# A graph and attention layer on one core: token chunks of 512, 512 and 226, counting windows in equal portions, and panel splits moved by one job

## The chip, the core and the metric

The kernel runs on one core of a Trainium2 chip. The time is the device time of one launch in microseconds (us), and lower is better. A core has five engines with queues of their own: TensorE (PE in the profile, with its weight loads shown as PEld), VectorE (DVE), ScalarE (ACT), GpSimd (POOL), and SyncE (SP), which here only issues DMAs. They wait for one another by semaphores. Matrix products go from SBUF to one of eight PSUM banks of 512 fp32 columns, and ACT or DVE take them out.

## What is computed

1250 tokens of 1024 numbers, 20000 edges (`src`, `dst`), fp32 in and out:

```python
xn = _layernorm(x)
x = x + gnn(xn, edge_index, W, b) + mix(xn, Wq, Wk, Wv, Wo, P)
x = x + ffn(_layernorm(x), Wg, Wu, Wd, Wr, temperature)
...
h = xn @ W.T + b                      # gnn: degree-normalised neighbour sum of h
out = segment_sum(norm[:, None] * h[col], row)
...
q', k' = relu(q P.T)/8, relu(k P.T)/8   # mix: 16 heads of 64, linear attention
attn = (q' @ (k'.T @ v)) @ Wo.T + bo
...
h = silu(x @ Wg[e]) * (x @ Wu[e])     # ffn: 8 experts of 128, weights w from a router
out = sum_e w[:, e] * (h @ Wd[e])
```

## The kernel before

**Products.** The tokens are padded to 1280 = 10 tiles of 128 (`NT`). An fp32 operand is kept as two fp32r parts, a high one (`xnH`, `w_hi`: a rounded copy, made by ACT) and a low one (`xnL`, `w_lo`: raw minus high, made by DVE or POOL), and a product is three matmuls for each of 8 slices of 128 rows: high by high, high by low, low by high. So one job that fills a PSUM bank is 24 matmuls. There are two forms. With tokens stationary (`rows`, L1525) the moving operand is 512 weight columns. With weights stationary (`columns`, L1653, and `expert`, L1789) the moving operand is a chunk of tokens, and `CHUNKS` cuts the 1250 tokens into three.

**Stages.** (1) Layer norm and the first value panel with 10 jobs `rows`. (2) Steps 10 to 39, one job `rows` each, for keys and values in two halves: in these steps the edge counts are made too. The 20000 edges are sorted by destination and lie in 157 chunks of 128. Window w of 32 destinations (`NWIN` = 40) takes `SHARE[w]` chunks for certain (25 for window 0, 11 for window 1, down to 3) and the rest, which depends on the data, in a loop (L1265, L1612). For each chunk DVE makes two one-hot matrices (`hot_pair`, L1253: 128x128 and 128x320, fp16) in a ring of 12, and PE multiplies them into bank 6 or 7 (L1608). A finished window is copied by ACT to `cw` (L897), added by POOL to `acc` (L728) and stored by SP. (3) 24 query jobs `columns(("q", j))`, chunk j % 3 each, interleaved with 8 products `fold` and then, from j = 8, with 16 products `mixed(g, h)` of three matmuls, for which Wo's eight row panels are loaded and split. (4) 20 jobs `rows` for H = xn W (`("h", hf, t)`). (5) Mixture and aggregation, 40 jobs with 512 columns. (6) The router and 48 jobs `expert(n, g)`, n = 0 to 23, three chunks for each of 8 experts, gate and up. (7) 20 jobs `down` with 512 columns.

**What sets the order.** Each engine's program is written out by hand. In stage 2 `_window_steps` (L48) deals whole windows to steps 11 to 39: a step takes windows until the chunks done reach its goal. DVE's step is: one-hots of the step's windows, then the result of the step's job (`k_out` or `v_out`), then a fold's low part. PE's is: the job, a fold, the windows, and then `kv` of the tile before. In stage 3 the jobs q and m (or fold) take banks 2 to 4 in turn, and a job waits until the job three before it has been drained (`free_bank`, L1521). ACT's turn j (L944 to L968) is `q_feature(j)`, which copies q_j out (L926) and rounds it (L929), then `m_high` (L942), and after odd j from 9 to 19 `wo_high(g + 2)` (L935), which waits for the DMA that SP issues in the same turn, after `m` has been drained (L497 to L499). POOL's turn is `q_low(j)`, then `wo_low`. H's first panel is split in four pieces after turns 14, 16, 18 and 20 (L854 on ACT, L682 on POOL). The second value panel is split at ACT's steps 10 to 13 and in POOL's call at L723, ahead of the first addition to `acc`.

## Time and profile before

| what | us |
|---|---|
| median of 3 runs | 1137.25 |
| lowest and highest | 1136.33, 1137.45 |
| the profiled execution | 1137.28 |
| its span (first to last instruction) | 1135.3 |
| PE busy | 1109.2 (98%) |
| ACT, POOL, DVE busy | 252.1, 295.7, 369.1 |
| TensorE's granted clock, mean | 0.995 |

The profiled execution took as long as the median of the runs, and 2.0 us of it lie outside the span. PE is busy for nearly the whole span, and a matmul counts as busy until its modelled end, so that several overlap: a busy share of 98% doesn't tell how densely they follow each other. That is read from their start times.

### The profile page before, as it was taken

Reading aid. Unit: us, or ns where it says so; the run is one execution under the profiler, and the core shown is the slowest. Engines: PE = TensorE matmul, PEld = TensorE weight load, DVE = VectorE, ACT = ScalarE, POOL = GpSimd, SP = SyncE. Lnnn points to the kernel's source line nnn. Section 1 sums busy time; section 2 is a strip of 40 time slices with the busy share of each in tenths; the row PEclk is TensorE's granted clock in tenths of the full one; section 3 lists DMA queues with packets and bytes.
Section 4 is the critical chain, followed back from the end, with each engine's and each line's share of the span. In section 5 each row is a group of like instructions: output and inputs, shape, how many; then the busy total and the mean of one; then the engine's idle time right before and its main releaser. Section 6 shows DMA issues by size and latency. Waiting matters only on the chain.

```text
span 1135.3 us, 15415 instructions
## 1 busy us (share of the span) xinstructions
PE 1109.2 (98%) x5707; PEld 955.6 (84%) x5707; DVE 369.1 (33%) x987; ACT 252.1 (22%) x398; POOL 295.7 (26%) x236
## 2 busy tenths in 40 slices
PE   5999999999999989999999999999999999999998
PEld 4885777878889988888878888887999999998887
DVE  6855256555542111142212223344321111111111
ACT  4331111112223234321111112334221111112000
POOL 6001201112123136330032443434132222225000
PEclk9998999999999999999999999999999999999999
DMA  6303001222233476713069996875022222216321
GB/s 238 112 29 102 12 19 53 67 59 63 71 92 103 159 254 226 241 55 149 1 188 298 312 262 192 240 222 159 1 84 60 60 60 60 68 53 213 103 100 67
DMA packets 144518, 139.29 MB, mean 123 GB/s; under 512 B 6636, under 2 KB 120636, under 8 KB 144189
## 3 DMA queue, kind: packets, MB, share of 16 engines
q1 hardware_dynamic: 143868, 136.20, 38.4%
q10 hardware_dynamic: 576, 2.10, 0.5%
q8 instruction: 48, 0.79, 0.3%
q14 instruction: 26, 0.20, 0.1%
HBM read 102.32 MB, written 35.96 MB: 122 GB/s over the span
## 4 chain that ended last, share of the span: by engine, by line
PE 93%; DMA 2%; DVE 2%; ACT 1%; issue 1%; SPq 0%; DVEq 0%; ACTq 0%
PE ps L1534 10%; PE ps L1535 10%; PE ps L1536 10%; PE ps L1800 7%; PE ps L1802 6%; PE ps L1801 6%; PE ps L1742 4%; PE ps L1736 4%; PE ps L1716 3%; PE ps L1717 3%; PE ps L1847 3%; PE ps L1718 3%; PE ps L1846 3%; PE ps L1848 3%; PE ps L1544 3%; PE ps L1659 2%
## 5 line engine op out<-in xcount | busy, mean ns | idle before, releaser
L1534 PE MATMUL ps<-w_hi,xnH 128*128 128x512 f32 x480 | 192.2, 400 | 0.0
L1536 PE MATMUL ps<-w_hi,xnL 128*128 128x512 f32 x480 | 187.9, 391 | 0.0
L1535 PE MATMUL ps<-w_lo,xnH 128*128 128x512 f32 x480 | 187.8, 391 | 0.0
L1534 PEld LDWEIGHTS ps<-w_hi,xnH 128*128 128x128 f32 x480 | 90.8, 189 | 19.7 <-POOL w_lo L682 0.3
L1536 PEld LDWEIGHTS ps<-w_hi,xnL 128*128 128x128 f32 x480 | 90.6, 189 | 19.5
L1535 PEld LDWEIGHTS ps<-w_lo,xnH 128*128 128x128 f32 x480 | 90.8, 189 | 17.7
L728 POOL TENSOR_TENSOR acc<-acc,cw 128x320 f32<-128x320 f32 x40 | 35.7, 892 | 171.5 <-ACT cw L897 170.6
L1659 PE MATMUL ps<-xnH,w_hi 128*128 128x416 f32 (+1 forms) x192 | 69.1, 360 | 3.1 <-DVE mL L1303 3.1
L1800 PE MATMUL ps<-x2H,guH 128*128 128x416 f32 (+1 forms) x192 | 68.1, 355 | 0.4 <-ACT wT L1077 0.4
L1802 PE MATMUL ps<-xnH,guL 128*128 128x416 f32 (+1 forms) x192 | 67.8, 353 | 0.0
L1801 PE MATMUL ps<-x2L,guH 128*128 128x416 f32 (+1 forms) x192 | 67.8, 353 | 0.0
L1801 PE MATMUL ps<-xnL,guH 128*128 128x416 f32 (+1 forms) x192 | 67.8, 353 | 0.0
L1800 PE MATMUL ps<-xnH,guH 128*128 128x416 f32 (+1 forms) x192 | 67.8, 353 | 0.0
L1802 PE MATMUL ps<-x2H,guL 128*128 128x416 f32 (+1 forms) x192 | 67.8, 353 | 0.0
L1661 PE MATMUL ps<-xnH,w_lo 128*128 128x416 f32 (+1 forms) x192 | 67.8, 353 | 0.0
L1660 PE MATMUL ps<-xnL,w_hi 128*128 128x416 f32 (+1 forms) x192 | 67.7, 353 | 0.0
L682 POOL TENSOR_TENSOR w_lo<-w_raw,w_hi 128x1024 fp32r<-128x1024 f32 x16 | 39.3, 2460 | 107.3 <-ACT w_hi L854 106.9
L1489 DVE TENSOR_TENSOR prd<-ps,wB 128x416 f32<-128x416 f32 (+1 forms) x24 | 14.2, 592 | 161.8 <-PE ps L1802 145.2
L1254 DVE TENSOR_SCALAR hot<-iota,key 128x128 f16<-128x128 f16 x178 | 54.6, 307 | 37.0 <-issue 31.6
L778 POOL TENSOR_TENSOR cL<-cR,cH 128x1280 fp32r<-128x1280 f32 x20 | 59.0, 2948 | 23.7 <-ACT cH L991 23.7
L1255 DVE TENSOR_SCALAR hot<-iota,key 128x320 f16<-128x320 f16 x178 | 55.9, 314 | 0.1
L773 POOL TENSOR_TENSOR xh<-xh,bob 128x512 f32<-128x512 f32 x10 | 12.9, 1288 | 135.1 <-DMA bob<-in 94.0
(312 smaller groups left out, 2050.3 us busy)
## 6 DMA issues: line engine op xcount, KB each, us to landing
cR<-c_d SPq DMA_DIRECT2D x20, 640.0 KB, 5.4
foldin<-in SPq DMA_DIRECT2D x32, 256.0 KB, 2.8
guR<-in SPq DMA_DIRECT2D x16, 512.0 KB, 5.4
c_d<-cw SPq DMA_DIRECT2D x40, 160.0 KB
w_raw<-in SPq DMA_DIRECT2D x12, 512.0 KB, 6.6
xb<-in SPq DMA_DIRECT2D x10, 512.0 KB, 4.9
qs0H<-qT_d SPq DMA_DIRECT2D x10, 512.0 KB, 5.3
qs0L<-qT_d SPq DMA_DIRECT2D x10, 512.0 KB, 6.3
```

Source lines behind the costliest of these rows:

```text
L778: pool.tensor_tensor(cL[k][:], cR[k][:], cH[k][:].bitcast(F32), ALU.subtract).then_inc(c_lo, 1)
L1254: dve.tensor_scalar(target1, iota[:, 0:P], key1[:, column], -512.0 * w, ALU.subtract, ALU.is_equal)
L1255: dve.tensor_scalar(target2, iota[:], key2[:, column], None, ALU.is_equal).then_inc(ready, 1)
L1534: pe.matmul(target, xnH[:, kc, cols], wH[w][:, kc, :], start=(kc == 0), stop=False)
L1535: pe.matmul(target, xnH[:, kc, cols], wL[w][:, kc, :], start=False, stop=False)
L1536: mm = pe.matmul(target, xnL[:, kc, cols], wH[w][:, kc, :], start=False, stop=(kc == KC - 1))
L1659: pe.matmul(target, wH[w][:, kc, block_cols], xnH[:, kc, first:last], start=(kc == 0), stop=False)
L1660: pe.matmul(target, wH[w][:, kc, block_cols], xnL[:, kc, first:last], start=False, stop=False)
L1661: mm = pe.matmul(target, wL[w][:, kc, block_cols], xnH[:, kc, first:last], start=False, stop=(kc == KC - 1))
L1800: pe.matmul(target, high, x2H(kc)[:, first:last], start=(kc == 0), stop=False)
L1801: pe.matmul(target, high, x2L(kc)[:, first:last], start=False, stop=False)
L1802: mm = pe.matmul(target, low, x2H(kc)[:, first:last], start=False, stop=(kc == KC - 1))
```

## The change

Four edits, all of them in order and sizes; the sums computed are the same.

1. `CHUNKS` is (0, 512), (512, 1024), (1024, 1250) instead of 418, 416 and 416 tokens. Tiles and addresses follow (cut from the diff). The stored width of the third query chunk is 256.
2. `_portions` deals the windows' chunks to the steps one by one: 7 or 8 in each step, with a window cut where the step's goal falls. `one_hots` and `window` get a begin and an end, and only the portion that ends a window runs the rest loop and the last matmul. SP's and ACT's work on a window stands in the step in which it ends.
3. The second value panel is rounded by ACT at steps 14 to 17 instead of 10 to 13, and its low part is made by DVE in these steps instead of by POOL.
4. `wo_high(g)` and `wo_low(g)`, g = 2 to 7, stand after turn 2g + 6 instead of 2g + 5 (so one q and one m later). H's pieces are split after turns 15, 17, 19 and 21 instead of 14, 16, 18 and 20.

```diff
-CHUNKS = ((0, 418), (418, 834), (834, 1250))
-QW = (418, 416, 446)
+CHUNKS = ((0, 512), (512, 1024), (1024, 1250))
+QW = (512, 512, 256)
...
+def _portions():
+
+    steps, w, n, last, done = {}, 0, 0, 4 * NT, 0
     total = SEEN[NWIN] + NWIN
-    done = 0
     for s in range(FIRST_WIN_STEP, last):
         goal = total * (s + 1 - FIRST_WIN_STEP) / (last - FIRST_WIN_STEP)
         steps[s] = []
-        while w < NWIN and (done < goal - 2 or s == last - 1):
-            steps[s].append(w)
-            done += SHARE[w] + 1
-            w += 1
+        while w < NWIN and (done < goal - 0.5 or s == last - 1):
+            stop = SEEN[w + 1] if s == last - 1 else min(SEEN[w + 1], n + max(1, round(goal - done)))
+            steps[s].append((w, n, stop))
+            done += stop - n
+            n = stop
+            if n == SEEN[w + 1]:
+                done, w = done + 1, w + 1
     return steps
...
@@ POOL
-            panel_lo(0)
+            split[0] += 4
             for w in range(NWIN):
...
             pool.wait_ge(hot_used, SEEN[NWIN])
+            pool.wait_ge(acc_step, NWIN)
+            for w in range(NWIN - 3, NWIN):
+                pool.wait_ge(c_st[w % 3], 16 * (w // 3 + 1))
...
-                if j >= KC and (j - KC) % 2 == 1 and (j - KC) // 2 + 2 < KC:
-                    wo_low((j - KC) // 2 + 2)
+                if j >= KC + 2 and (j - KC) % 2 == 0 and (j - KC) // 2 + 1 < KC:
+                    wo_low((j - KC) // 2 + 1)
...
-                if j in (14, 16, 18, 20):
-                    panel_lo(0, ((j - 14) // 2,))
+                if j in (15, 17, 19, 21):
+                    panel_lo(0, ((j - 15) // 2,))
...
@@ ACT
-                if s < NT + 4:
-                    panel_hi(0, t, 2)
+                if NT + 4 <= s < NT + 8:
+                    panel_hi(0, t - 4, 2)
...
-                    if h == 1 and g + 2 < KC:
-                        wo_high(g + 2)
+                    if h == 0 and g >= 1 and g + 1 < KC:
+                        wo_high(g + 1)
...
-                if j in (14, 16, 18, 20):
-                    panel_hi(0, (j - 14) // 2, 3)
+                if j in (15, 17, 19, 21):
+                    panel_hi(0, (j - 15) // 2, 3)
...
@@ DVE
-            def one_hots(w):
+            def one_hots(w, begin, end):
                 first = dve.value_load(rng[0:1, 0, w:w + 1], min_val=0, max_val=NCH - 1)
...
-                for n in range(SEEN[w], SEEN[w + 1]):
+                for n in range(begin, end):
...
+                if end < SEEN[w + 1]:
+                    return
...
-                for w in WINDOWS.get(s, ()):
-                    one_hots(w)
+                for portion in PORTIONS.get(s, ()):
+                    one_hots(*portion)
+                if NT + 4 <= s < NT + 8:
+                    kcs = slice(2 * (t - 4), 2 * (t - 4) + 2)
+                    dve.wait_ge(pan_hi, t + 1)
+                    dve.tensor_tensor(wL[0][:, kcs, :], wR[0][:, kcs, :], wH[0][:, kcs, :].bitcast(F32), ALU.subtract)\
+                       .then_inc(pan_lo, 1)
...
@@ PE
-            def window(w):
+            def window(w, begin, end):
...
-                for n in range(SEEN[w], SEEN[w + 1]):
+                for n in range(begin, end):
...
+                if end < SEEN[w + 1]:
+                    return
```

The first place is PE at step 11 (program order; L1534 to L1536 are a `rows` job, L1608 the one-hot products, L1615 the rest loop's, L1619 the window's last matmul, L1629 `kv`). Before, all 25 chunks of window 0 stand there, with its end:

```order
L1536 MATMUL ps<-w1_hi_66,xnL_64 128x512
L1608 MATMUL ps<-hot2_93,hot1_92 128x320 x25
...
L1615 MATMUL ps<-rest2_97,rest1_96 128x320
...
L1619 MATMUL ps<-shifted_104,idq_103 128x320
L1629 MATMUL ps<-ktmp_95,vst_71 64x64 x8
L1534 MATMUL ps<-w1_hi_66,xnH_63 128x512
```

Now (the same code, lines L1549 to L1551 and L1623; L1646 is `kv`), in the same step and the next:

```order
L1551 MATMUL ps<-w1_hi_66,xnL_64 128x512
L1623 MATMUL ps<-hot2_93,hot1_92 128x320 x8
L1646 MATMUL ps<-ktmp_95,vst_71 64x64 x8
L1549 MATMUL ps<-w1_hi_66,xnH_63 128x512
...
L1551 MATMUL ps<-w1_hi_66,xnL_64 128x512
L1623 MATMUL ps<-hot2_93,hot1_92 128x320 x7
L1646 MATMUL ps<-ktmp_95,vst_71 64x64 x8
```

Window 0 is now spread over steps 11 to 14 (8, 7, 8 and 2 chunks), and its end stands in step 14.

The second place is ACT in turns 11 and 12 of the query stage (qF and qH are the feature and its rounded copy of chunk 0, 1 or 2; mH is `m_high`, woH `wo_high`). Before:

```order
L942 ACTIVATE mH_127<-ps 128x512
L935 ACTIVATE woH1_134<-woR1_130 128x1024
L926 ACTIVATE qF0_116<-ps,bqf_61 128x418
L929 ACTIVATE qH0_122<-qF0_116 128x418
L942 ACTIVATE mH_127<-ps 128x512
L926 ACTIVATE qF1_117<-ps,bqf_61 128x416
```

Now:

```order
L949 ACTIVATE mH_127<-ps 128x512
L933 ACTIVATE qF0_116<-ps,bqf_61 128x512
L936 ACTIVATE qH0_122<-qF0_116 128x512
L949 ACTIVATE mH_127<-ps 128x512
L942 ACTIVATE woH1_134<-woR1_130 128x1024
L933 ACTIVATE qF1_117<-ps,bqf_61 128x512
```

The rounding of Wo's panel 3 stood ahead of q_12's copy and now stands behind it and behind m_12.

## Rows read from the trace of the kernel before

**Rows 1.** The page, busy time and clock in 40 slices (engine, us, share, instructions)
```profile
PE 1109.2 (98%) x5707; PEld 955.6 (84%) x5707; DVE 369.1 (33%) x987; ACT 252.1 (22%) x398; POOL 295.7 (26%) x236
PEclk9998999999999999999999999999999999999999
```

**Rows 2.** Stretches of step 11: us, busy (count), then granted clock, DMA
```profile
100.00:106.50 6.50, 5.84 (x24) 2.79 (x22) 6.50 (x26) 0.00 (x0) 1.83 (x1) 1.00 0.22 67
106.50:116.70 10.20, 8.81 (x37) 4.35 (x37) 5.20 (x26) 1.99 (x3) 1.32 (x1) 0.51 0.04 11
```

**Rows 3.** Timeline of step 11: start, duration, engine, line [idle before]
```profile
99.41 2.47 DVE L1254 TENSOR_SCALAR hot<-iota,key 128x128 f16<-128x128 f16 x1
99.44 2.40 POOL L682 TENSOR_TENSOR w_lo<-w_raw,w_hi 128x1024 fp32r<-128x1024 f32 x1 [0.38 <-ACT w_hi L854]
...
102.02 0.24 DVE L1254 TENSOR_SCALAR hot<-iota,key 128x128 f16<-128x128 f16 x1
...
102.20 9.03 PE L1608 MATMUL ps<-hot,hot 128*128 128x320 f16 x25
...
102.39 0.24 DVE L1254 TENSOR_SCALAR hot<-iota,key 128x128 f16<-128x128 f16 x1
...
112.56 0.45 PE L1615 MATMUL ps<-rest,rest 128*128 128x320 f16 x1 [1.33 <-issue]
...
116.99 0.40 PE L1534 MATMUL ps<-w_hi,xnH 128*128 128x512 f32 x1
```

**Rows 4.** Timeline of PE elsewhere: `kv` and a one-hot burst without waits
```profile
121.21 0.69 PE L1629 MATMUL ps<-ktmp,vst 128*64 128x64 f32 x16
121.83 0.50 PE L1534 MATMUL ps<-w_hi,xnH 128*128 128x512 f32 x1
...
209.05 0.71 PE L1608 MATMUL ps<-hot,hot 128*128 128x320 f16 x4
209.59 0.30 PE L1615 MATMUL ps<-rest,rest 128*128 128x320 f16 x1
```

**Rows 5.** Waits of PE in the whole span: us, times, longest
```profile
PE ps L1659 <- DVE mL L1303: 3.1, 5, 0.8
...
PE ps L1671 <- ACT qF L926: 1.9, 2, 1.7
```

**Rows 6.** Timeline of the query stage, the longest of these waits
```profile
417.22 0.59 SPq L469 DMA_DIRECT2D woR<-in  x1
...
422.92 1.06 ACT L935 ACTIVATE woH<-woR 128x1024 fp32r<-128x1024 f32 x1 [9.29 <-DMA woR<-in]
423.89 0.59 ACT L926 ACTIVATE qF<-ps,bqf 128x416 f32<-128x416 f32 x1
...
424.53 0.50 PE L1671 MATMUL ps<-woH,kvH 128*128 128x512 f32 x1 [1.68 <-ACT qF L926]
```

**Rows 7.** One expert (six jobs) on PE: us, PE busy (count), clock, DMA
```profile
857.30:884.91 27.61, 27.61 (x145) 1.00 0.21 62
```

**Rows 8.** The down stage, all engines as in Rows 2
```profile
1023.40:1132.00 108.60, 108.56 (x479) 89.56 (x478) 14.16 (x21) 6.81 (x7) 15.28 (x7) 1.00 0.36 124
```

**Rows 9.** Weight loads by form (count, busy us, mean ns)
```profile
L1544 PEld LDWEIGHTS ps<-pbd_s,foldin 128*128 128x128 f32 x256 | 32.9, 191 | 1.4
...
L1765 PEld LDWEIGHTS ps<-x2H,wrs 128*16 128x16 f32 x12 | 1.1, 95 | 1.1
```

**Rows 10.** Timeline of PE: short plain-fp32 matmuls, each with its 128x128 load
```profile
31.89 1.95 PE L1554 MATMUL ps<-bqc,pbd_s 128*128 128x1 f32 x16
33.70 1.14 PE L1544 MATMUL ps<-pbd_s,foldin 128*128 128x128 f32 x8
34.59 0.47 PE L1534 MATMUL ps<-w_hi,xnH 128*128 128x512 f32 x1
```

**Rows 11.** Timeline around a late one-hot in step 28
```profile
246.15 0.25 DVE L1254 TENSOR_SCALAR hot<-iota,key 128x128 f16<-128x128 f16 x1 [2.01 <-issue]
...
248.95 0.31 PE L1615 MATMUL ps<-rest,rest 128*128 128x320 f16 x1 [0.97 <-issue]
```

More of the change, by code:

```diff
@@ L43 @@
 FIRST_WIN_STEP = NT + 1
-CHUNKS = ((0, 418), (418, 834), (834, 1250))
-QW = (418, 416, 446)
-def _window_steps():
-    steps, w, last = {}, 0, 4 * NT
+CHUNKS = ((0, 512), (512, 1024), (1024, 1250))
+QW = (512, 512, 256)
+def _portions():
+    steps, w, n, last, done = {}, 0, 0, 4 * NT, 0
     total = SEEN[NWIN] + NWIN
-    done = 0
     for s in range(FIRST_WIN_STEP, last):
@@ L54, in _window_steps @@
         steps[s] = []
-        while w < NWIN and (done < goal - 2 or s == last - 1):
-            steps[s].append(w)
-            done += SHARE[w] + 1
-            w += 1
-    return steps
-WINDOWS = _window_steps()
+        while w < NWIN and (done < goal - 0.5 or s == last - 1):
[5 more added lines that the diff above has]
+                done, w = done + 1, w + 1
+    return steps
+PORTIONS = _portions()
+WINDOWS = {s: [w for w, n, stop in parts if stop == SEEN[w + 1]] for s, parts in PORTIONS.items()}
 def _job_ids():
@@ L168, in gps_layer @@
             ("bqc", [P, KC], F32), ("acc", [P, SRCG], F32)), OP, OC)
[L171 to L177 removed]
+        qF = [at(f"qF{c}", [P, QW[c]], F32, OY + 4096 * c) for c in range(3)]
+        qL = [at(f"qL{c}", [P, QW[c]], F32R, OY + 4096 * c) for c in range(3)]
+        qH = [at(f"qH{c}", [P, QW[c]], F32R, OY + 4096 * c + 4 * QW[c]) for c in range(3)]
+        kvH = at("kvH", [P, KC, P], F32R, OY + 10240)
+        kvL = at("kvL", [P, KC, P], F32R, OY + 14336)
+        mH = at("mH", [P, 2, W], F32R, OY + 18432)
+        mL = at("mL", [P, 2, W], F32R, OY + 22528)
         woR = [at(f"woR{p}", [P, D], F32, OH + 8192 * p) for p in range(2)]
@@ L622, in load_wb @@
                 first, last = CHUNKS[c]
-                sp.dma_start(wB[:, n % 2, 0:last - first], wx_d[e:e + 1, first:last].to_broadcast([P, last - first]))\
+                sp.dma_start(wB[n % 2][:, 0:last - first], wx_d[e:e + 1, first:last].to_broadcast([P, last - first]))\
                   .then_inc(in_wb[n % 2], 16)
@@ L1643, in _ @@
                     fold(s // NT - 1, t - 1)
-                for w in WINDOWS.get(s, ()):
-                    window(w)
+                for portion in PORTIONS.get(s, ()):
+                    window(*portion)
                 if s // NT % 2 and t:
```

22 lines of the change are left out of this document (8 added, 14 removed).

## Prediction

> **What bounds the kernel now.** I read the page's busy times first: PE is busy for 1109.2 of 1135.3 us, no other engine for more than 370, and the granted clock is full in all slices but one or two [rows 1]. So PE's own sequence sets the end, and a gain has to come from one of two things: stretches in which PE stands or runs slowly, or matmuls that follow each other more densely. Both have to be looked for by start times, since the busy share hides them. Three places bear on this change.
>
> First, step 11. The stretches show DVE busy all the time up to 106.5 while PE's weight loads fill 2.79 of 6.50 us, and after that a mean clock of 0.51, which is the 1.2 GHz level, for about 10.2 us [rows 2]. The timeline shows why: the 25 one-hot products of window 0 take from 102.20 to past 111, because DVE delivers a pair in 0.37 us (102.02 to 102.39), and then the rest loop's product waits for 1.33 us more. The clock fell while PE was being fed like this, and it was back for the matmul at 116.99 [rows 3]. DVE had no lead either: its one-hot at 99.41 took 2.47 us while POOL split a piece of the value panel from 99.44 to 101.84 [rows 3].
>
> Second, the query stage. PE's waits list 3.1 us for DVE's mL in five waits and 1.9 us for ACT's qF in two [rows 5]. In the longest one ACT sat for 9.29 us in front of the rounding of a Wo panel whose DMA SP had issued at 417.22; only then could it copy q out (423.89), and PE, which had waited for that, went on at 424.53 [rows 6].
>
> Third, all jobs that stream tokens. One expert is 144 matmuls in 27.61 us, 191.7 ns each at a mean of 416.7 columns [rows 7]. In the down stage 479 matmuls of 512 columns took 108.6 us, 226.7 ns each [rows 8]. 95.3 columns for 35.0 ns is 0.37 ns per column; at 2.4 GHz a column is 0.417 ns, so 512 is 13.4 ns over its columns and the chunks of 416 are 18.1 ns over theirs. The wide form is the cheaper one per column.
>
> **The change part by part.** *Step 11.* From 102.20 to 116.99 PE spent 14.8 us [rows 3]. Fed in time, the same work is 25 one-hot products at 0.135 us (four in 0.54 us) = 3.4, the rest and last products 0.3, `kv` 0.6 (121.21 to 121.83), and six matmuls of the next job at 0.227 = 1.4, together 5.7 us [rows 4, 8]. The loss is 9.1 us. After the change 8 products stand there, 1.1 us, and the other 17 go to steps 12 to 14, at 0.135 us each as before. DVE needs 8 x 0.37 = 3.0 us for its 8 pairs; it began 0.7 us before 99.41, so it ends by 101.7 and PE arrives at 102.2. The POOL piece that held it up is gone. In later steps DVE has a whole job of PE (24 x 0.227 = 5.4 us) for 7 or 8 pairs, and the ring of 12 holds them. With no starved stretch I expect no 1.2 GHz stretch. Gain 9.1; if DVE should still be 1.5 us late at step 11, 7.6. I take 9.1.
>
> The moved panel split itself: four DVE subtractions of 128x1024. The nearest DVE row is 0.24 us for 128 fp16 columns, which says little; POOL's 2.40 for the same shape [rows 3] is the upper bound, also for how long k's addition behind it on DVE is put off. They run in steps 14 to 17 between one-hots and `k_out`, both of which have PE's job of 5.4 us as cover: 3.0 + 2.4 fills it just about, so I take 0 and keep up to 1 us for the range. PE needs the panel at step 20 only. POOL loses 4 x 2.4 us ahead of its additions, which nobody waits for there.
>
> What happens on DVE with POOL is told by one place of the Trainium skill (SBUF — State Buffer, section Who interferes with whom): whichever of a 2-port VectorE operation and a GpSimd operation comes first keeps the shared port pair for its whole duration. The pair at 99.41 agrees. The same section says that a VectorE instruction with two SBUF inputs also contends with a GpSimd one that reads SBUF, and the four moved subtractions are such; by it they could now meet POOL's additions to `acc`, some 0.9 us at a time, which would stay within the 1 us kept above.
>
> *Window portions.* Cutting windows adds some twenty partial portions, each with one more load of a register on DVE. Steps with three portions now exist. DVE's idle pieces show the risk: it began a pair at 246.15 after 2.01 us in which it waited for nothing the profile shows, and PE lost 0.97 us by it [rows 11]. That place may vanish, and one or two others may come. I take +1.2 us; bounds -1 and +3.
>
> *Wo's panels.* The rounding now has a whole further turn (a q of up to 5.4 us and an m of 0.7) before ACT reaches it. The longest landing is 422.92 - 417.22 = 5.7 us [rows 6]. Where the turn behind is the short chunk (226 columns, 2.7 us and 0.7) ACT still stands for 2 to 4 us, but then PE is in a 512 chunk and needs ACT only at its end. `wo_low` and `m` of the panel come two turns later, 11 us on average, for 1.06 on ACT and some 2.4 on POOL. H's pieces move to turns without a Wo panel, so no turn has both. SP's queue is unchanged in order. So the 5.0 us of [rows 5] go; what is late next is q's store, behind which the copy of three turns later waits, with about 15 us for it. I take -5.0, bounds -6 (some of the loss lies under the modelled ends of matmuls) and -3.
>
> *Chunks.* There are 8 x 3 x 8 = 192 matmuls for each chunk in the query stage and 384 in the experts, 576 sets of three. A set costs 3 x 191.7 = 575 ns now. The two of 512 cost 226.7 each [rows 8]. No fp32r matmul under 384 columns is in the trace, so the one of 226 has to be bounded. Its columns with the 13.4 ns of the wide form: 94.2 + 13.4 = 107.6. Its weight load: a load of 128 columns is shown with 191 ns and one of 16 with 95 ns [rows 9], so 0.86 ns per column and 110 for 128; and sixteen matmuls of one column with such loads follow each other at 1.81/16 = 113 ns, eight of 128 columns at 0.89/8 = 111 [rows 10]. So the load, not the columns, sets the short one: 113 ns, nearest to the row with the shortest matmul. Set: 2 x 226.7 + 113 = 566.4, 8.8 ns less, x 576 = -5.1 us. Bounds: 107.6 for the short one gives -8.2 us; 121 for it (a load and the 13.4 ns besides) with wide ones at 229 gives +2.3.
>
> Sum: 1137.28 - 9.1 - 5.0 - 5.1 + 1.2 = 1119.3 us; the profiled execution is that of the median. The other parts (PSUM copies of 512 instead of 416 columns, and products with `wB`) lie beside jobs of 5.4 us with four bank pairs between.
>
> The Trainium skill (TensorE: Matmul & The Clock Gate, sections Back-to-back issue gap and LDWEIGHTS) has a rule against the chunks. It gives a gap of N/2.4 + 2.5 ns and a load of columns/1.2, so 107 ns for 128. By it three even chunks are 528 ns and the new ones 2 x 215.8 + 106.7 = 538: an estimate of +5.8 us for 576 sets, because the short chunk pays for its load. The rows have 575 and not 528, so the even chunks pay for something that this rule lacks.
>
> **The rivals.** *A: the overhead of the even chunks belongs to the operands.* If the 18.1 ns come with tokens and these weights as operands, whatever the width, the 512 chunks pay them too: 231.4, and the short one 113: 576 ns, so no gain from edit 1. Then 1137.28 - 9.1 - 5.0 + 1.2 = 1124.4; with the load's charge of the page's rule it would be up to 1130. For it: the wide rows are from other operands. Against it: nothing in the form of the instructions differs but the width.
>
> *B (slower): the short fp32r matmul is far dearer.* Either it runs at the rate of the fold's plain fp32 matmuls (two instructions of 111 ns for 128 columns [rows 10], 1.74 ns per column, 393 for 226), or it waits out the whole shown duration of its load (191 ns [rows 9]). The first makes a set 847 ns, +156 us, 1281 us in all; the second 645, +40 us, 1164. Place: every third query and expert job. It decides from the point where the set is 23 + 8.8 ns dearer than forecast, a short matmul of about 145 ns. For it: no such matmul was ever seen in this trace. Against it: fp32 loads follow each other at 111 to 113 ns, and the streams are of the same 4-byte data.
>
> *C: the starved stretch moves.* Portions of three windows in a step put DVE at its limit, and PE waits a little in each of ten steps (0.5 us): 1119.3 + 5 = 1124. Or Wo's wait is replaced by one for q's stores. For it: 2.01 us of DVE without a cause [rows 11]. Against it: 8 pairs are 3.0 us of a step of some 7.5.
>
> **How the numbers follow.** Forecast 0.66, with a range of its own from 1112 to 1124 (all lower bounds but the noise: -9.1 - 6 - 8.2 - 1 = 1113; upper: 7.6, 3, half of the chunk term, +2). A 0.12, C 0.12, B 0.10, of which the fp32 rate is 0.06. The predicted time is 1119. The range 1112 to 1129 takes in A and C and leaves out B and strays. A measurement of this kernel can tell some 0.2% (2.3 us) from no change. Faster by more than that: forecast, A and C, 0.89; within it 0.01; slower 0.10.
>
> **What would show it.** Step 11: no DVE-fed burst, a clock of 1.00 through 100 to 120, one-hot products at 0.135 us. Query stage: no wait of PE for mL or qF over 0.5 us, `woH` waiting less than 4 us. Chunks: six jobs of an expert in about 27.2 us, short matmuls 107 to 121 ns apart, wide ones 227. The text is wrong if a short one is over 145 ns, if the 1.2 GHz stretch stays or comes elsewhere, or if the wide ones start 231 ns apart.

## The result and the profile after

The changed kernel takes 1121.04 us (median of 4 runs, 1120.78 to 1122.03), the kernel before beside it 1137.35 (1136.33 to 1139.73): a ratio of 0.9857, interval 0.9845 to 0.9868, 16.3 us less where 18 were forecast. The profiled execution is one of 1121.14 us with a span of 1119.2.

The page, as [rows 1]:

```profile
PE 1098.6 (98%) x5707; PEld 911.8 (81%) x5707; DVE 369.6 (33%) x991; ACT 252.9 (23%) x398; POOL 287.5 (26%) x232
PEclk9999999999999999999999999999999999999999
```

The slice with an 8 at step 11 is gone. The stretches, as [rows 2, 7]; the third is one expert:

```profile
100.00:106.50 6.50, 6.50 (x45) 4.95 (x45) 4.89 (x23) 0.72 (x1) 0.00 (x0) 1.00 0.25 75
106.50:116.70 10.20, 10.20 (x61) 8.02 (x60) 3.79 (x17) 0.72 (x1) 0.00 (x0) 1.00 0.01 2
843.86:871.02 27.16, 27.16 (x147) 23.38 (x146) 3.78 (x6) 4.77 (x8) 8.12 (x7) 1.00 0.22 63
```

Step 11 now runs 45 and 61 matmuls where 24 and 37 ran, all at 2.4 GHz, and POOL is silent there. An expert takes 27.16 us where it took 27.61. All waits of PE of 0.5 us and more behind the start, as [rows 5], then the eight one-hot products of step 11:

```profile
PE ps L1632 <- issue: 2.1, 3, 1.3
PE ps L1733 <- DVE htmp L1351: 0.8, 1, 0.8
PE ps L1769 <- ACT xt L1012: 0.6, 1, 0.6
PE ps L1646 <- ACT ktmp L908: 0.5, 1, 0.5
```

```profile
102.33 1.26 PE L1623 MATMUL ps<-hot,hot 128*128 128x320 f16 x8
```

Not one wait for mL or qF is left; L1632 is the rest loop's product. A new loss stands in none of these lists. Here is the timeline of PE behind q's first job, where the degrees (12 products of one column, each two plain-fp32 matmul instructions, so 24 rows) and a fold run:

```profile
332.01 0.39 PE L1678 MATMUL ps<-xnH,w_lo 128*128 128x512 f32 x1
332.24 0.50 PE L1698 MATMUL ps<-qmask,acc 128*128 128x1 f32 x4
332.67 0.28 PE L1701 MATMUL ps<-qmask,acc 128*64 128x1 f32 x4
332.88 1.05 PE L1698 MATMUL ps<-qmask,acc 128*128 128x1 f32 x8
...
334.54 1.83 PE L1559 MATMUL ps<-pbd_s,foldin 128*128 128x128 f32 x8
336.03 0.77 PE L1676 MATMUL ps<-xnH,w_hi 128*128 128x512 f32 x1
336.60 0.63 PE L1677 MATMUL ps<-xnL,w_hi 128*128 128x512 f32 x1
```

The wide matmuls at 336.03 and 336.60 are 0.57 us apart where others are 0.227: the granted clock is at 1.2 GHz from 334.79 for 3.41 us, and it was from 324.55 for 3.41 us too.

To see where the time went I take, from both traces, the start of the first matmul of each stage and subtract. The same is done for the experiments, so it stands in one table (us; "falls" gives the starts of the stretches at 1.2 GHz, with their lengths; the one with which each trace ends, which begins in the last 1.4 us of the span or behind it, is left out). The columns are the stages between the first one-hot product, q's first matmul, m's first, h's first, the first expert's, the second expert's and the first of the down stage; between h and the first expert nothing moves in any kernel (325.9 us, within 0.1), nor does the down stage. What lies ahead of the first one-hot product is not counted; its start differs by up to 1.2 us between traces (102.16 to 103.32).

| kernel | windows | q to m | m to h | first expert | other experts | falls |
|---|---|---|---|---|---|---|
| before | 231.02 | 51.02 | 86.50 | 33.33 | 193.05 | 106.76 (10.24) |
| changed | 223.17 | 53.18 | 78.88 | 33.27 | 190.20 | 324.55, 334.79 (3.41 each) |
| Wo only | 230.90 | 51.02 | 79.82 | 33.33 | 193.05 | 106.64 (10.24) |
| portions only | 223.99 | 51.02 | 86.94 | 33.33 | 193.05 | none |
| panel only | 228.81 | 51.02 | 86.12 | 33.33 | 193.05 | 109.36 (6.83) |
| chunks only | 231.86 | 50.43 | 87.20 | 34.92 | 190.20 | 108.88 (10.24), 815.44 (3.41) |
| changed + probe | 223.21 | 50.44 | 78.88 | 34.87 | 190.20 | 797.74 (3.41), 1118.59 (10.24, ahead of the probe) |
| even, aligned | 222.21 | 52.13 | 78.88 | 34.72 | 190.33 | 324.56, 795.60 (3.41 each) |
| 512/496/242 | 223.06 | 50.27 | 78.22 | 34.73 | 188.45 | 797.27 (3.41) |
| light last step | 221.78 | 52.01 | 78.88 | 34.85 | 190.20 | 332.68, 796.89 (3.41 each) |
| thin ones spread | 222.97 | 51.30 | 78.88 | 34.47 | 190.22 | none |
| all together | 221.58 | 51.08 | 78.22 | 34.36 | 188.45 | none |
| halves | 221.60 | 52.56 | 78.22 | 35.15 | 188.48 | none |

Changed minus before: -7.85, +2.16, -7.62, -0.06, -2.85, in sum -16.2.

How well does a stage repeat? Six of these traces (changed, its repetition with 223.30, changed + probe, even and aligned, 512/496/242, thin ones spread) have the same code up to q's first job, and their windows stage takes 222.21 to 223.30 us; with the windows of before it is 230.90 to 231.86. So one trace against another settles nothing under some 1 us there. The stages behind it repeat within 0.1 us as long as no fall lies in them, but for m to h where PE still waits for Wo's panels: there three kernels with the same code have 86.12 to 86.94 us.

### The profile page after: what moved, and what is told of

Read it like the earlier page. It is cut to its first block, busy times and chain, and to the rows that moved or that the text cites. A ratio compares the mean times of both kernels' runs of the same rounds, so it can differ in the third digit from the quotient of the medians.

```text
span 1119.2 us, 15481 instructions
## 1 busy us (share of the span) xinstructions
PE 1098.6 (98%) x5707; PEld 911.8 (81%) x5707; DVE 369.6 (33%) x991; ACT 252.9 (23%) x398; POOL 287.5 (26%) x232
## 4 chain that ended last, share of the span: by engine, by line
PE 97%; DVE 1%; ACT 1%; DMA 1%; issue 0%; POOL 0%; DVEq 0%
PE ps L1549 10%; PE ps L1551 10%; PE ps L1550 10%; PE ps L1817 7%; PE ps L1819 6%; PE ps L1818 6%; PE ps L1759 4%; PE ps L1753 4%; PE ps L1676 3%; PE ps L1677 3%; PE ps L1678 3%; PE ps L1733 3%; PE ps L1865 3%; PE ps L1735 3%; PE ps L1734 3%; PE ps L1864 3%
## 5 line engine op out<-in xcount | busy, mean ns | idle before, releaser
L1549 PE MATMUL ps<-w_hi,xnH 128*128 128x512 f32 x480 | 191.4, 399 | 0.2 <-POOL w_lo L686 0.2
L1551 PE MATMUL ps<-w_hi,xnL 128*128 128x512 f32 x480 | 187.2, 390 | 0.0
L1549 PEld LDWEIGHTS ps<-w_hi,xnH 128*128 128x128 f32 x480 | 90.3, 188 | 19.8 <-POOL w_lo L686 0.7
L1551 PEld LDWEIGHTS ps<-w_hi,xnL 128*128 128x128 f32 x480 | 90.2, 188 | 19.4
L1676 PE MATMUL ps<-xnH,w_hi 128*128 128x512 f32 (+1 forms) x192 | 69.2, 360 | 0.0
L1677 PE MATMUL ps<-xnL,w_hi 128*128 128x512 f32 (+1 forms) x192 | 68.3, 356 | 0.0
L1678 PE MATMUL ps<-xnH,w_lo 128*128 128x512 f32 (+1 forms) x192 | 68.0, 354 | 0.0
L1817 PE MATMUL ps<-x2H,guH 128*128 128x512 f32 (+1 forms) x192 | 67.6, 352 | 0.4 <-ACT wT L1084 0.4
L1818 PE MATMUL ps<-x2L,guH 128*128 128x512 f32 (+1 forms) x192 | 67.6, 352 | 0.0
L1819 PE MATMUL ps<-x2H,guL 128*128 128x512 f32 (+1 forms) x192 | 67.5, 352 | 0.0
L1817 PE MATMUL ps<-xnH,guH 128*128 128x512 f32 (+1 forms) x192 | 67.5, 351 | 0.0
L1819 PE MATMUL ps<-xnH,guL 128*128 128x512 f32 (+1 forms) x192 | 67.4, 351 | 0.0
L1818 PE MATMUL ps<-xnL,guH 128*128 128x512 f32 (+1 forms) x192 | 67.3, 350 | 0.0
L998 ACT ACTIVATE cH<-cR 128x1280 fp32r<-128x1280 f32 x20 | 25.4, 1272 | 98.0 <-DMA cR<-c_d 98.0
```

The lines of the kernel that those rows point to most:

```text
L1549: pe.matmul(target, xnH[:, kc, cols], wH[w][:, kc, :], start=(kc == 0), stop=False)
L1551: mm = pe.matmul(target, xnL[:, kc, cols], wH[w][:, kc, :], start=False, stop=(kc == KC - 1))
L1676: pe.matmul(target, wH[w][:, kc, block_cols], xnH[:, kc, first:last], start=(kc == 0), stop=False)
L1677: pe.matmul(target, wH[w][:, kc, block_cols], xnL[:, kc, first:last], start=False, stop=False)
L1678: mm = pe.matmul(target, wL[w][:, kc, block_cols], xnH[:, kc, first:last], start=False, stop=(kc == KC - 1))
L1817: pe.matmul(target, high, x2H(kc)[:, first:last], start=(kc == 0), stop=False)
```

## The experiments

All times below are medians, and each ratio is to the kernel before on the same chip. The microseconds gained follow from the ratio; it is not quite that of the two medians, by which the four single edits gain more (7.6 us for edit 4, 5.3 for edit 2, 3.7 for edit 3 and 3.1 for edit 1).

**One edit at a time.** Edit 4 alone; beside these lines its twins in ACT's and POOL's code:

```
-                    if h == 1 and g + 2 < KC:
-                        wo_high(g + 2)
+                    if h == 0 and g >= 1 and g + 1 < KC:
+                        wo_high(g + 1)
...
-                if j in (14, 16, 18, 20):
-                    panel_hi(0, (j - 14) // 2, 3)
+                if j in (15, 17, 19, 21):
+                    panel_hi(0, (j - 15) // 2, 3)
```

> The kernel before with edit 4 alone (Wo's rounding one turn later on ACT and POOL, H's pieces in odd turns). Forecast: the waits of PE for mL and qF (5.0 us in seven waits, rows 5) go and nothing takes their place: 1137.3 - 5.0 = 1132.3 (1131.3 to 1134.3). The two traces give 7.6 us between q's first and h's first matmul for edits 1 and 4 together, of which edit 1 has 192/576 of its own sum: if edit 1 is worth 5.1 in all, 1.7 of the 7.6 is its, and 5.9 is edit 4's: 1131.4. Rival (the short chunk is what removes the wait, since PE reaches ACT's copies later in a 512 chunk): with even chunks a wait for qF or mL of over 2 us stays, and the gain is under 3 us: above 1134.3.

1131.26 against 1138.83 us, ratio 0.9941 (0.9924 to 0.9957), 6.7 us less. The stage from m to h is shorter by 6.68, the rest stands. The profile's list has no wait for mL or qF left, with even chunks. So the edit needs no short chunk; the rival falls.

Edit 2 alone, the planner and its two users (the same in `window`):

```
-                for w in WINDOWS.get(s, ()):
-                    one_hots(w)
+                for portion in PORTIONS.get(s, ()):
+                    one_hots(*portion)
```

> The kernel before with edit 2 alone (the windows cut into portions; the value panel's low half still split by POOL in steps 11 to 13, where it held DVE up at 99.41). Forecast: portions are the cause, since 8 pairs are enough to do before PE comes: DVE may still be up to 1.5 us late under POOL's split, so 1137.3 - 7.6 + 1.2 = 1130.9, and with the new end of step 39 (three windows, whose loss I read as about 4 us in the changed kernel, 1.2 of which is in the 1.2) some 1129 to 1132; no stretch at 1.2 GHz at step 11. Rival P (the pair of edits is needed: POOL's split holds DVE's shared port so that PE starves at step 11 with 8 pairs too and the clock falls): a stretch at 1.2 GHz of some 10 us between 100 and 120 stays and the time is 1134 or more.

1133.54 us, ratio 0.9957 (0.9942 to 0.9971), 4.9 less. Its profile, with POOL's split still in place (a stretch of all engines and, from the timeline of DVE, the pair that meets that split):

```profile
100.00:120.00 20.00, 19.74 (x131) 14.35 (x130) 16.77 (x49) 4.07 (x5) 6.58 (x3) 1.00 0.07 22
```

```profile
99.42 2.47 DVE L1259 TENSOR_SCALAR hot<-iota,key 128x320 f16<-128x320 f16 x1
```

The stage is 7.03 us shorter at a clock of 1.00 although DVE still stands for 2.47 us under POOL's split: rival P falls, the smaller share of window 0 is what feeds PE. (POOL's split is recorded from 99.40 here and from 99.44 in the kernel before, DVE's instruction from 99.42 and 99.41; which of the two came first is too close to tell. They end within 0.1 us of each other.) The profiled run is the kernel's fastest (1130.61); its five runs have 1130.61, 1131.26, 1133.54, 1133.87 and 1135.04 us at mean clocks of 1.000, 0.998, 0.997, 0.995 and 0.995. Those 4.4 us go with the clock, so this kernel has falls too in most runs, and its median gains some 2 us less than its profiled run.

Edit 3 alone:

```
-            panel_lo(0)
+            split[0] += 4
...
+                if NT + 4 <= s < NT + 8:
+                    dve.tensor_tensor(wL[0][:, kcs, :], wR[0][:, kcs, :], wH[0][:, kcs, :].bitcast(F32), ALU.subtract)\
+                       .then_inc(pan_lo, 1)
```

> The kernel before with edit 3 alone (the value panel's split moved from POOL in steps 11 to 13 to DVE and ACT in steps 14 to 17; window 0 whole in step 11). Forecast: 0 to -1: DVE's 2.47 us pair at 99.41 becomes 0.37, so DVE is 2.1 us earlier, but PE reaches step 11 at 102.20 and then still takes pairs at DVE's 0.37 each, of which the ring holds 12 at most: with (102.2 - 98.7)/0.37 = 9 pairs ready the other 16 take 5.9 us in place of 9.2, so -2 to -3 us if the clock stays up or falls as before; 1134.3 to 1136.3. Rival P: the panel is the cause of the starved stretch: the clock stays at 2.4 GHz and most of 7.8 us goes: 1130 or less. Rival Q: the four subtractions on DVE delay k's additions and one-hots behind them: slower, 1138 to 1139.

1135.18 us, ratio 0.9971 (0.9961 to 0.9980), 3.3 less; the stage is 2.2 shorter and the fall 6.83 us long, not 10.24.

```profile
103.32 6.79 PE L1613 MATMUL ps<-hot,hot 128*128 128x320 f16 x25
```

The 25 products take 6.79 us where they took 9.03 and would take 3.4 if fed in time. That is the forecast of this run, not P or Q: DVE gets a lead of some pairs and PE starves for the rest. Beside edit 2 the panel brings less, since both remove the same stretch: from step 11's job to step 12's there are 7.25 us in the changed kernel and 8.33 with the portions alone, 1.1 us, and 0.8 over the whole stage (223.17 against 223.99), which is inside what two traces can differ by.

Edit 1 alone, with the buffers and the memset's waits that go with it:

```
-CHUNKS = ((0, 418), (418, 834), (834, 1250))
-QW = (418, 416, 446)
+CHUNKS = ((0, 512), (512, 1024), (1024, 1250))
+QW = (512, 512, 256)
```

> The kernel before with edit 1 alone (chunks of 512, 512 and 226, their buffers, the memset's waits). By the two traces' groups of 24: a set of three is 577 ns in the experts and 579 in q's jobs before, 566 and 569 after: 10 to 11 ns x 576 = 6 us at most; the stages' starts gave 0.6 up to m's first matmul, 0.9 to h's and 3.3 in the experts, 4.8 in all. Forecast (prediction's term): 5.1 faster, with PE's waits for mL and qF as before or somewhat changed (the ring of Wo turns is the same): ratio 0.9955. Rival to the reading of the Wo-only run (that the chunks alone take away part of those waits): the stage from m's first matmul to h's is shorter than the 86.5 of before by more than 2 us; if the two are independent, by 0.9. Rival R (the short turn brings ACT's and POOL's work of a turn into 2.7 + 0.7 us, so the waits for Wo grow when its rounding is not moved): the stage is longer than 86.5 and edit 1 alone gains under 3 us.

1134.53 us, ratio 0.9974 (0.9965 to 0.9983), 3.0 less, against 5.1. The profiled run is the slowest of the eleven, with 1137.99 us: its windows stage is 0.8 longer than before though PE and DVE have no edit there, and it has a fall of 1.6 us, so its stages do not add up to the gain of the median. They show each part all the same, and the profile's waits of PE the middle one:

```profile
PE ps L1662 <- DVE mL L1306: 3.2, 4, 1.0
PE ps L1674 <- ACT qF L929: 2.9, 4, 2.0
```

Seven waits of 5.0 us in all [rows 5] have become eight of 6.1, and the stage from m to h is 0.7 longer than before, although its own jobs are 0.9 shorter: rival R, whose other sign, a gain under 3 us, is met only just (2.96 by the ratio, 3.1 by the medians). And the first expert has 1.6 us more by a fall at 815.44, where the kernel before has none in its profile. With the Wo edit in place the same stage loses nothing, so edit 4 is worth 6.7 us beside even chunks and 8.3 (87.20 to 78.88) beside the new ones.

**What a width costs.** A probe behind the end of the changed kernel:

```
+            pe.wait_ge(d_dr, 2 * NT)
+            for n, off in PROBE:
+                for i in range(24):
+                    pe.matmul(bank(i % 2, n), d1H[:, i % 8, i % 4 * P:(i % 4 + 1) * P], xnH[:, i % 4, off:off + n], start=True,
+                              stop=True)
```

> The changed kernel with, after its last output block is summed, 44 groups of 24 more fp32r matmuls on PE (stationary 128x128 out of the down panel, moving N columns of fp32r from x2, into two banks in turn): N from 128 to 512 at offset 0, then 416 columns at offsets 2 to 834, 512 at 2 to 514, and the chunks' own (226 at 1024, 242 at 1008, 418 at 832, 496 at 512). The outputs are the reference's; only the time behind the outputs is new. What is read is the distance of starts in each group. Theory L: the distance is the greater of 112 ns and N/2.4 + 13.4, wherever the columns begin: 226 and 232 at 112, 256 at 120, 320 at 147, 384 at 173.4, 416 at 186.7 for every offset, 418 at 187.6, 512 at 226.7. Theory U: columns are taken in units of 8 or 16 and a cut unit is paid whole: 416 at offset 418 or 834 takes 190 to 193, 418 at 0 takes 190, 512 at offset 2 takes 230 to 233. Theory C: the 190 to 193 ns of the even chunks come from what runs beside them (the other engines), so here, where nothing runs, 416 takes 186.7 at every offset and 418 takes 187.6, as in L, but the same chunks in the kernel stay at 190 to 193 also from aligned starts. Rival A of the prediction (the overhead belongs to the operands, not the width): 512 in this group differs from the 226.7 of the down stage.

It ran once, with 1311.18 us, and its trace is read for the groups alone. Stretches of PE, each from the first start of one group of 24 to that of the next (us, PE busy, clock, DMA share, GB/s); in order 226, 256, 384, 416 and 512 columns from 0; then 416 from 416, from 418, from 832 and from 834; 512 from 512 and from 514; and 242 from 1008:

```profile
1129.22:1131.91 2.69, 2.69 (x27) 1.00 0.00 0
1140.04:1142.90 2.86, 2.86 (x27) 1.00 0.00 0
1153.42:1157.58 4.16, 4.16 (x26) 1.00 0.00 0
1170.82:1175.34 4.52, 4.52 (x25) 1.00 0.01 4
1214.84:1220.31 5.47, 5.47 (x26) 1.00 0.00 0
1247.55:1252.03 4.48, 4.48 (x25) 1.00 0.01 4
1252.03:1256.67 4.64, 4.64 (x26) 1.00 0.00 0
1256.67:1261.19 4.52, 4.52 (x25) 1.00 0.00 0
1261.19:1265.79 4.60, 4.60 (x25) 1.00 0.00 0
1282.57:1288.03 5.46, 5.46 (x25) 1.00 0.00 0
1288.03:1293.64 5.61, 5.61 (x25) 1.00 0.00 0
...
1296.31:1299.04 2.73, 2.73 (x27) 1.00 0.00 0
```

A 24th of each: 112, 119, 173, 188, 228; 187, 193, 188, 192; 228, 234; 114 ns. So 226 and 240 columns cost the same 112 (the groups of the probe that stand in no row here are read from the same trace in the same way). Above that theory L holds in part: 320 columns took 146.6 ns, 352 160.0, 384 173.5 and 400 180.0, which is 0.417 ns for each column and 13.3 over them. Beside that the start of the columns counts: 416 from 418 and 512 from 514 are 6 to 7 ns dearer than from 416 and from 512. And some widths are dear from 0 as well: 418 took 189.8, 424 193.3, 432 195.8, 448 206.3, 496 223.5 and 504 226.8, where 13.3 over the columns would be 187.5, 190.0, 193.3, 200.0, 220.0 and 223.3; 496 from 512 took 220.0. That is U's direction, but not its rule: 416 columns from 4 took 186.8, from 8 193.4, from 12 187.1 and from 16 188.3. Which starts and widths are dear is seen, not explained. C falls, since nothing runs beside the probe and the dear starts are dear here too, and rival A of the prediction with it: other operands, same 227.7.

The Trainium skill (TensorE: Matmul & The Clock Gate, section Back-to-back issue gap) has N/2.4 + 2.5 ns and no word on the start of the columns; these rows have 13.3 and more in place of 2.5, and the estimate of +5.8 us for the change that the prediction worked out from it, with 173 + 2.5 for the even chunks, was wrong in sign. Its section LDWEIGHTS gives columns/1.2, so 107 ns for 128; the floor of 112 is near it.

**Is it the width or the cut?** Even chunks from better starts, in the changed kernel:

```
-CHUNKS = ((0, 512), (512, 1024), (1024, 1250))
+CHUNKS = ((0, 416), (416, 832), (832, 1250))
...
```

> The changed kernel with even chunks again, but cut at multiples of 416: columns 0, 416 and 832 (416, 416, 418 wide; q's buffers laid out by the same cuts). Theory W (the prediction's: even chunks pay 18.1 ns over their columns because of their width): a set of three is 575 ns as before the change, 9.7 ns more than now: slower than the changed kernel by 576 x 9.7 = 5.6 us. Theory M (the start of the columns: in the probe 416 columns took 193.2 from offset 418 and 191.8 from 834, but 188.2, 186.8 and 190.0 from 0, 416 and 832): 565.0 ns, the same as 2 x 226.7 + 111.7 = 565.1 of the changed kernel: within 1 us of it.

1120.83 us, ratio 0.9851 (0.9836 to 0.9867); the changed kernel on the same chip had 1120.17, 0.9841 (0.9828 to 0.9854), from this run:

> The changed kernel once more, on the same chip as the next three, so that they can be held against it directly. Both theories: ratio to before 0.9845 to 0.9868. On the clock: theory F (falls are struck by chance among the places with short or late matmuls): the profile has its short 1.2 GHz stretches at other places than 324.55 and 334.79, in sum 3 to 7 us. Theory S (the three windows of step 39 make the fall): the fall is at 324.5 again.

The two are the same, and the other experts take 190.33 and 190.20 us. Theory W, the one of the prediction, falls: even chunks are no worse than 512, 512, 226. What the kernel before paid for was that two of its three chunks began at 418 and 834: by the probe its three chunks are 189.8 + 193.1 + 191.7 = 574.6 ns, and those from 0, 416 and 832 are 188.3 + 186.8 + 190.4 = 565.5. As for the clock, the repeated run has its falls at 324.55 and 334.79 again. But the changed kernel with the probe, the same code up to its end, has neither of the two and one at 797.74 instead, and the even chunks have theirs at 324.56 and 795.60. So the places recur, and which of them a run meets is not fixed by the code. The two theories of the clock are each half wrong, and the next runs go on.

**Using the floor.** Chunks (0, 512), (512, 1008), (1008, 1250):

> The changed kernel with chunks of 512, 496 and 242 columns (from 0, 512, 1008). Theory L (a matmul takes the greater of the load's 112 ns and its columns with 13.4 ns, so the short chunk has room up to some 237 columns): by the probe 227.6 + 220.0 + 113.4 = 561.0, by the kernel's own wide groups 226.7 + 220.0 + 113.4 = 560.1, against 565.1: 5.0 ns x 576 = 2.9 us faster than the changed kernel: 0.26% less. Rival (the probe's widths do not hold with three operands in turn, or the waits for Wo's panels come back as the short chunk changes): within 1 us of the changed kernel.

1118.30 us, ratio 0.9829 (0.9813 to 0.9844), 1.9 less than the changed kernel beside it, with intervals that overlap; the stages say it more sharply: 0.66 less from m to h and 1.75 less in the other experts (7 experts with 48 sets of one matmul of each chunk, so 5.2 ns for a set where 5.0 were expected).

**The last step of the windows.** One number of the planner:

```
-        goal = total * (s + 1 - FIRST_WIN_STEP) / (last - FIRST_WIN_STEP)
+        goal = total * (s + 1 - FIRST_WIN_STEP) / (last - FIRST_WIN_STEP - 0.75)
```

> The changed kernel with the window portions planned to end 0.75 of a step earlier: step 39 then ends one window and has one one-hot product, in place of three windows and five products. Theory S (step 39's three windows cost PE 1.25 + 0.5 + some 0.4 us of waits, and the clock fell because of them: 3.4 + 3.4 us at 1.2 GHz, 3.4 us lost): 4 to 5 us faster than the changed kernel, and no 1.2 GHz stretch near 324. Theory F (the waits are lost there, the clock falls by chance, also elsewhere): 1 to 2 us faster (0.1 to 0.2%), and the sum of 1.2 GHz stretches unchanged. Rival N (the waits move to step 38, whose windows come closer together): no change.

1118.14 us, ratio 0.9824 (0.9811 to 0.9837), 2.0 less than the changed kernel beside it, again with overlapping intervals. The windows stage is 1.4 to 1.5 us shorter than in that kernel's two traces (221.78; the two later kernels with this planning have 221.58 and 221.60). In the changed kernel the end of step 39 is this:

```profile
321.24 0.31 PE L1623 MATMUL ps<-hot,hot 128*128 128x320 f16 x1
322.80 0.31 PE L1632 MATMUL ps<-rest,rest 128*128 128x320 f16 x1 [1.25 <-issue]
...
324.48 1.09 PE L1646 MATMUL ps<-ktmp,vst 128*64 128x64 f32 x16 [0.52 <-ACT ktmp L908]
```

The wait of 1.25 us is gone with the light last step, as theory F had it; the one of 0.52 stays. But the falls do not vanish, they stand at 332.68 and 796.89. The timeline of PE at the second:

```profile
794.48 0.39 PE L1819 MATMUL ps<-xnH,guL 128*128 128x512 f32 x1
794.79 2.55 PE L1790 MATMUL ps<-ones,zTs 16*128 16x8 f32 x20
797.27 0.80 PE L1817 MATMUL ps<-x2H,guH 128*128 128x512 f32 x1
```

Ten products of 8 columns, each two instructions, take 2.5 us, and the clock is at 1.2 GHz at their end. The kernel before has the same products, and no fall there in its profile. In the five traces with a fall near 797 (or 815) these ran just ahead of it; in the three at 332.7 to 334.8 the 24 instructions of one column and a fold; at 324.55 the last one-hots and 32 kv instructions of 64 columns, with waits between.

**Breaking the thin runs up.** In `columns` and `expert` the thin products go behind single steps of the wide ones:

```
-                columns(("q", j), m, c, m // 4)
-                if j == 0:
-                    degrees()
+                columns(("q", j), m, c, m // 4, degrees() if j == 1 else None)
...
-            expert(0, 1)
-            logits()
+            expert(0, 1, logits())
```

> The changed kernel with two runs of thin matmuls spread between wide ones: the 23 one-column products of the degrees (131 ns apart, behind q's first job) go one to three at a time behind the steps of q's second job, and the 20 products of 8 columns of the router's sums (behind the first expert's second job) go in pairs of t between that job's last matmuls. Work and data are the same. Theory T (the 1.2 GHz stretches at 332 to 338 and at 794 to 801 come from these runs of thin matmuls: in the three traces that show the one at 797 the 20 products of 8 columns ran just before it, in the one of 332.68 the 23 of one column): no such stretch at either place, one at 324.55 may stay; the time is 1.5 to 3 us below the changed kernel's (ratio to before 0.9815 to 0.983) and its spread over runs smaller. Rival F (the falls are struck by chance over the whole kernel): stretches of 3.4 to 6.8 us in sum stay, elsewhere; no change (0.984). Rival H (a thin matmul between wide ones costs more than in a run: PE changes the bank and the shape): slower by up to 43 x 0.1 = 4 us.

The clock is 1.000 in all five runs, and in all five of the next kernel, which is spread too; of the 24 runs of the changed kernel and of the three variants of it above, one has 1.000. So theory T is right on the cause for the two places that it named. The fall at 324.55 is missing as well, but it lies ahead of the first edited job: of the six traces with the same code up to there three have it and three do not, and what brings it is not shown. And the time is the same: 1120.38 us, ratio 0.9846 (0.9833 to 0.9860), so theory T's gain is not there. The timeline of PE tells where it went:

```profile
333.24 0.28 PE L1704 MATMUL ps<-qmask,acc 128*64 128x1 f32 x2
333.44 0.50 PE L1676 MATMUL ps<-xnH,w_hi 128*128 128x512 f32 x1
333.78 0.39 PE L1677 MATMUL ps<-xnL,w_hi 128*128 128x512 f32 x1
334.01 0.40 PE L1678 MATMUL ps<-xnH,w_lo 128*128 128x512 f32 x1
334.34 0.28 PE L1704 MATMUL ps<-qmask,acc 128*64 128x1 f32 x2
```

The second wide matmul begins 0.34 us behind the first, the third 0.23 behind the second: the first wide one behind thin ones costs about 0.1 us more. In the first expert it is more than that one gap:

```profile
794.01 0.39 PE L1826 MATMUL ps<-xnH,guL 128*128 128x512 f32 x1
794.33 0.61 PE L1795 MATMUL ps<-ones,zTs 16*128 16x8 f32 x4
794.87 0.50 PE L1824 MATMUL ps<-xnH,guH 128*128 128x512 f32 x1
795.21 0.39 PE L1825 MATMUL ps<-xnL,guH 128*128 128x512 f32 x1
```

The thin ones begin 0.32 us behind the last wide one (0.09 over the usual), the next wide one 0.18 behind the last thin one (0.07 over), and the wide one after it 0.34 behind that (0.11 over). Against the same stages without a fall, q to m has 51.30 where 50.44 was seen, with four groups of degrees, so 0.21 us for each, and the first expert 34.47 where 33.27 was, with five groups of sums, 0.24 for each: 2.1 us, rival H at half its price. The falls cost 2.7 from q to m in the changed kernel (53.18 against 50.44).

**All three together:**

> The changed kernel with the three findings together: chunks of 512, 496, 242 (2.9 us less by the probe; its own run had 1118.3 against 1120.2), the windows planned 0.75 of a step earlier (1.5 us in the stage's length; 1118.1 against 1120.2), and the thin matmuls spread (1.5 to 3 us if theory T holds). If they add: 1120.2 - 2.9 - 1.5 - 2.0 = 1113.8 (ratio 0.978 to 0.979), with no 1.2 GHz stretch before the end. If the falls cannot be removed: 1115.8.

1116.37 us (1116.03 to 1116.85), ratio 0.9815 (0.9801 to 0.9828), clock 1.000 in all runs: 3 to 5 us below the changed kernel by its two ratios on other chips (0.9841, 0.9857), and the fastest here. It misses 1113.8 by about what the spreading costs.

**Fewer changes from thin to wide,** on top of the new chunks and the light last step (`deg` and `sums` are the two runs of thin products, each stopping once at half):

```
-                if j == 0:
-                    degrees()
+                if j == 0:
+                    deg = degrees()
+                if j < 2:
+                    next(deg, None)
...
-            logits()
+            sums = logits()
+            next(sums, None)
             for n in range(1, 3):
                 for g in range(2):
                     expert(n, g)
+                    if n == 1 and g == 0:
+                        next(sums, None)
```

> As the kernel with the three findings together, but the thin matmuls are not spread: each of the two runs is only cut in half (the degrees of five tiles behind q's first job and of five behind its second; the router's sums of five tiles behind the first expert's second job and of five behind the job after it). Theory G (what the spreading cost was each change from thin to wide: in the spread kernel the first wide matmul behind a group of thin ones was followed after 314 to 339 ns where others are after 227 to 236; 13 such groups, 2.1 us lost in the two stages): four groups in place of 13 lose some 0.3 us more than two, so 1.2 to 1.8 us less than in the spread kernel: 1114.6 to 1115.2 (ratio 0.980), if a half is short enough to leave the clock up. Rival D (the cost is per thin matmul that stands in another place): no change, 1116.4. Rival E (a half still lets the clock fall): 1.2 GHz stretches at 330 to 340 or 793 to 800 come back, 1.6 us each, the mean clock of the runs is 0.998 again, and the time is 1115.5 to 1118 with a wider spread.

1119.53 us, ratio 0.9831 (0.9816 to 0.9846): by 1.8 us slower than the spread one on another chip (by 3.0 us in the profiled spans), which none of the three foresaw. The expectation counts 13 groups in the spread kernel; its trace has nine, four of degrees and five of sums. The clock is 1.000 in three runs and 0.998 in two. PE's waits, which the spread one does not have:

```profile
PE ps L1559 <- DMA foldin<-in: 2.1, 1, 2.1
PE ps L1843 <- DVE wexp L1493: 1.5, 1, 1.5
```

SP waits for `deg_mm` ahead of all that it issues in this stage. The degrees end at 338.7 now, and SP's next issues show it:

```profile
338.76 0.33 SPq L492 DMA_DIRECT2D bhb<-in  x1
339.13 0.44 SPq L400 DMA_DIRECT2D foldin<-in  x1
```

The first is issued at 332.14 in the light-last kernel; so the third fold's input comes late. The router's weights end one job later too, for 1.5 us. Beyond these waits, q to m is 0.2 us longer than the 50.27 of the 512/496/242 kernel, and the first expert 0.4 longer than without a fall, where the kernel with all three lost 0.8 and 1.1. That would be 1.3 us saved by five groups fewer, so G's saving seems to be there, at about the 0.2 to 0.24 us for a group from above; but it is argued by taking 3.6 us of new waits off, and no run shows it alone. Two of the five runs have a clock of 0.998, so rival E is right for some runs.

## Why the prediction was right or wrong

**Step 11.** Right in cause, place and size. The starved stretch and its 1.2 GHz are gone, DVE has its eight pairs ready at 102.33 (the products run in 1.26 us). Forecast -9.1 + 1.2 = -7.9 for the stage, measured -7.85, with up to 1 us between traces of the same code, so that the hit to 0.05 is luck. The two terms can be told apart all the same: with a light last step the stage is 9.2 us shorter than before, and the 1.4 between are the portions' cost, nearly all of it in the three windows of step 39. The starts of the jobs say so too: the changed kernel leads by 9.97 us at the start of step 39's job and by 7.85 at q's first matmul. The prediction looked for that at the place of [rows 11] and spread over many steps (rival C); it is one step, and one that the planner's table shows. Giving the panel no gain of its own was wrong as a statement on edit 3, which has 2.2 us alone; beside edit 2 it has some 1 us at step 11. Its cost of 0 was right: the four moved subtractions take 1.22 us each on DVE, where the bound was 2.40.

**The clock.** "With no starved stretch I expect no 1.2 GHz stretch" failed, and cost 2.7 us in the profiled run. By the prediction's own sign (it is wrong if the stretch "stays or comes elsewhere") this step is wrong. The prediction priced a fall only where PE starves. The clock falls behind runs of thin products as well. These stood at full clock in the one trace that the prediction read, but in 28 of 47 later runs of the kernel before the mean clock is 0.992 to 0.994, below the 0.995 of that trace, so it seems to have such falls too, and no trace shows where. This is the largest error in the sum.

**Wo's panels.** Right in mechanism, mis-sized: 6.7 us alone and 8.3 beside the new chunks, where I took 5.0 and a bound of 6. The waits list counts only gaps at the modelled ends of matmuls, and I kept 1 us for what lies under them; it was 1.7, beyond the bound. That the short turn would have made the waits longer without this edit was named in no step.

**Chunks.** Sum -5.1, measured -0.6 from q to m, -0.9 from m to h (79.82 to 78.88) and -2.9 in the experts: -4.4. The short matmul at 111.4 ns in the experts and the wide one at 226.7 in most groups (227 to 228 on average) are as forecast. In the other experts the old set is 574.6 ns (193.05 us for 336 sets) and the new one 566.1, so 8.5 of the 8.8 are there; in q's jobs it is 8, and in the first expert only 0.06 us came where 0.4 were due, which is not explained. But the reading behind it, "The wide form is the cheaper one per column", was wrong: three even chunks from better starts cost the same, and the old ones paid for where they began. The prediction hit the number because it took both prices from rows of the same widths and starts.

**The rivals.** A falls by the probe. B's price (145 ns) is far from 112. C was right in kind for one step. The range and the signs held: what failed up (falls, +2.7; chunks, +0.7) was partly met by Wo's 1.7 more, and that 16.3 us came so near to 18 is in part this luck.

## What to carry to other kernels

Before costing a tile shape, take the matmul's pitch from groups that differ in width and in start separately: here equal shares cut at 416 and 832 do as well as 512, 512, 226, and a short remainder costs the same 112 ns up to some 240 columns. A run of thin matmuls is a place where the clock may fall, in one run and not in the next of the same code, so compare kernels by the lengths of their stages and their falls, and never by one of them; and take a stage's length from more than one trace. Moving work past a semaphore that a DMA queue waits for moves the whole queue.

## What was unexpected of the hardware

- The start of a matmul's fp32 columns costs up to 6.6 ns in 187: 416 columns took 186.8 ns from 416, 193.1 from 418 and 193.4 from 8; 512 took 227.7 from 512 and 233.8 from 514. Some widths are dear from 0 too: 448 took 206.3 ns, 6.3 more than 13.3 over its columns.
- With a 128x128 fp32 load for each, matmuls of 226, 232 and 240 columns have the same pitch, 112.0, 111.8 and 112.2 ns.
- Twenty matmul instructions of 8 columns, 2.5 us long, were followed by 3.41 us at 1.2 GHz in some runs, for about 1.6 us; spreading the thin ones between wide ones kept 2.4 GHz in all ten runs of two kernels, and gave it back in 0.21 to 0.24 us for each of nine groups.
